# Writing expert results without a read-modify-write, and summing them in a last pass

## The reference

```python
h = tok(x, ...)                                   # 8 x 512 tokens, 192 features
h = h + attn(layernorm(h), ...)
h = h + ffn(layernorm(h), Wg, W1, b1, W2, b2)

def ffn(x, Wg, W1, b1, W2, b2):
    gate_scores = einsum('bsd,de->bse', x, Wg)
    topk_scores, topk_idx = top_k(gate_scores, 2)
    topk_probs = softmax(topk_scores)
    h = gelu(einsum('bsd,edh->bseh', x, W1) + b1)  # 8 experts, 384 hidden
    y = einsum('bseh,eho->bseo', h, W2) + b2
    y_sel = take_along_axis(y, topk_idx[..., None], axis=2)
    return sum(topk_probs[..., None] * y_sel, axis=2)
```

## Time and profile before

| what | value |
|---|---|
| median of 3 runs | 338.76 us (336.81 to 340.1) |
| span of the profiled execution | 338.6 us |
| POOL busy | 250.2 us (74%) |
| PE busy | 240.9 us (71%) |
| DVE busy | 177.6 us (52%) |
| ACT busy | 95.2 us (28%) |
| DMA moved | 22.61 MB |

### The profile page before, as it was taken

One profiled execution on the slowest core, in us unless ns is written; L12 is line 12 of the kernel. 1 busy time (PEld: TensorE's weight loads), 2 busy tenths in 40 slices (PEclk: granted clock), 3 DMA queues, 4 the chain that ended last, 5 costly groups with the idle time before them and its releaser, 6 DMA issues. The chain is left out here.

```text
span 338.6 us, 6221 instructions
## 1 busy us (share of the span) xinstructions
PE 240.9 (71%) x1585; PEld 162.0 (48%) x1585; DVE 177.6 (52%) x698; ACT 95.2 (28%) x223; POOL 250.2 (74%) x283
## 2 busy tenths in 40 slices
PE   0831973668478989768654899999999587999500
PEld 0621641223243445444421678777777365877400
DVE  5758997488998866684699322232222122122200
ACT  1002001354324144634233323332432132133000
POOL 5778979309968777766777388888883888888673
PEclk9999995558955556965555599999999799699955
DMA  6710019900000001111123146656461556564510
GB/s 191 201 13 11 0 45 400 382 5 2 2 0 9 12 13 60 63 57 60 59 70 103 22 54 69 64 62 67 53 69 18 60 62 65 61 69 50 59 10 0
DMA packets 28141, 22.61 MB, mean 67 GB/s; under 512 B 15434, under 2 KB 25546, under 8 KB 27787
## 3 DMA queue, kind: packets, MB, share of 16 engines
q0 software_dynamic: 13296, 7.95, 21.1%
q1 hardware_dynamic: 14524, 14.23, 13.0%
q10 hardware_dynamic: 288, 0.03, 0.1%
HBM read 7.25 MB, written 15.63 MB: 68 GB/s over the span
## 5 line engine op out<-in xcount | busy, mean ns | idle before, releaser
L709 POOL DMA_INDIRECT out<-up x71 | 110.3, 1554 | 33.1 <-issue 13.9
L1972 PE MATMUL bank_b<-down,up 128*128 x426 | 91.2, 354 | 5.0 <-DVE up L1473 1.0
L1972 PEld LDWEIGHTS bank_b<-down,up 128*128 128x128 f32 x426 | 72.9, 200 | 22.6 <-issue 18.8
L1473 DVE TENSOR_SCALAR up<-bank_b,up 128x192 f32<-128x192 f32 x71 | 29.6, 418 | 97.5 <-PE bank_b L1972 84.9
L657 POOL DMA_INDIRECT routed<-rows,slot x64 | 61.9, 968 | 23.9 <-issue 18.0
L472 POOL DMA_INDIRECT theta_all<-angles,ids x32 | 32.4, 1012 | 10.9 <-issue 9.0
L1651 ACT ACTIVATE up<-bank_a 128x384 f32<-128x384 f32 x71 | 31.3, 497 | 3.4 <-PE bank_a L1962 2.9
L1775 PE MATMUL bank_b<-queries_t,keys_t 32*128 32x512 f32 x64 | 26.1, 900 | 6.9 <-ACT keys_t L1499 3.4
L1782 PE MATMUL bank_a<-keys_t,wt 32*128 32x512 f32 x64 | 27.6, 949 | 3.8 <-DVE nmax L1133 2.1
L1663 ACT COPY up<-bank_c 128x384 f32<-128x384 f32 x18 | 8.6, 478 | 61.8 <-PE bank_c L1951 58.7
L1133 DVE TENSOR_REDUCE nmax<-bank_a 128x2 f32<-128x1024 f32 x16 | 19.5, 1219 | 11.5 <-PE bank_a L1782 11.3
(11 more groups left out here) (420 smaller groups left out, 369.4 us busy)
## 6 DMA issues: line engine op xcount, KB each, us to landing
routed<-pad_rows SPq DMA_DIRECT2D x8, 528.0 KB, 5.7
out<-hres SPq DMA_DIRECT2D x8, 384.0 KB, 2.4
down<-down_w SPq DMA_DIRECT2D x1, 2304.0 KB, 11.9
up<-up_w SPq DMA_DIRECT2D x1, 1536.0 KB
out<-up POOLq DMA_INDIRECT x71, 3.5
up<-routed SPq DMA_DIRECT2D x69, 16.0 KB
routed<-rows,slot POOLq DMA_INDIRECT x64
up<-up_w SPq DMA_DIRECT2D x1, 780.0 KB
```

The costliest lines, as they stand in the source:

```text
L709: pool.indirect_dma_start(out=out_rows, out_offset=bass.IndirectOffsetOnAxis(xb[:, m // STEP % RING, m % STEP, DEST:DEST + 1].bitcast(I32) ...
L1473: dve.tensor_scalar(y[:, m % RESULTS, :], bank_b[:, m % 2, 0:D], xb[:, m // STEP % RING, m % STEP, SHARE:SHARE + 1], None, ALU.mult).then_ ...
L1972: mm = pe.matmul(bank_b[:, m % 2, 0:D], hid[:, m % STEP, c * P:(c + 1) * P], down[:, bass.ds(first + c * D, D)], start=(c == 0), stop=(c = ...
```

## The change

The two rows of a token no longer meet in one place. A new buffer `results` in device memory has one row per token and choice (8192 rows), and 1024 spare rows for the rows of blocks that no token filled. POOL's DMA is a plain indirect write into it, with no add, no bounds check and no order between blocks. The destination that travels with a row is now `k * TOKENS + token`, and DVE takes the smaller of it and a spare row for each block (`target`, one column of 128 numbers). At the end SP loads all of `results` back, batch by batch (`back`, 16 transfers of 128 partitions by 768 numbers, 384 KB each), DVE adds the two rows and the residual (two additions of 128x768 per batch), and SP stores the batch. The stores of `hres` during attention are gone, since `out` is now written once, at the end.

The order computation on DVE is gone (18 instructions after the block table, and one in it). SP loads a block of the ring when DVE has scaled the old one (`y_done`), where it waited for the landing of that block's add. The circuits' tables move into the room of `back`, which is not used until the end; their instructions are the same. POOL has one more index table to fill early (`spare`).

```diff
             for m in range(BLOCKS):
-                last_shared = pool.value_load(t_i[0:1, 1, m:m + 1], min_val=1, max_val=BLOCKS + 1)
                 pool.wait_ge(y_done, m + 1)
-                pool.wait_ge(landed, last_shared)
-                hold(pool)
                 pool.indirect_dma_start(
-                    out=out_rows, out_offset=bass.IndirectOffsetOnAxis(
-                        xb[:, m // STEP % RING, m % STEP, DEST:DEST + 1].bitcast(I32), 0),
-                    in_=y[:, m % RESULTS, :], in_offset=None, bounds_check=TOKENS - 1,
-                    oob_is_err=False, compute_op=ALU.add).then_inc(added[m % RESULTS], 16)
+                    out=results, out_offset=bass.IndirectOffsetOnAxis(target[:, m % RESULTS:m % RESULTS + 1], 0),
+                    in_=y[:, m % RESULTS, :], in_offset=None).then_inc(added[m % RESULTS], 16)
...
             def weighted(m):
                 dve.wait_ge(y_mm, m + 1)
                 if m >= RESULTS:
                     dve.wait_ge(added[m % RESULTS], 16 * (m // RESULTS))
+                dve.tensor_tensor(target[:, m % RESULTS:m % RESULTS + 1],
+                                  xb[:, m // STEP % RING, m % STEP, DEST:DEST + 1].bitcast(I32),
+                                  spare[:, m % RESULTS:m % RESULTS + 1], ALU.min)
...
+            dve.wait_ge(h2_copied, 2 * BATCHES)
+            for b in range(BATCHES):
+                dve.wait_ge(back_in[b], 32)
+                step(dve.tensor_tensor(back[:, b, 0, :], back[:, b, 0, :], back[:, b, 1, :], ALU.add))
+                join()
+                dve.tensor_tensor(hres[:, b, :], hres[:, b, :], back[:, b, 0, :], ALU.add).then_inc(summed, 1)
...
-            for m in range(BLOCKS):
-                sp.wait_ge(added[m % RESULTS], 16 * (m // RESULTS) + 16)
-                sp.sem_inc(landed, 1)
-                if m + RING * STEP < BLOCKS:
-                    load_block(m + RING * STEP, block_row(m + RING * STEP))
-            sp.wait_ge(h2_out, 16 * BATCHES)
+            for m in range(BLOCKS - RING * STEP):
+                sp.wait_ge(y_done, m + 1)
+                load_block(m + RING * STEP, block_row(m + RING * STEP))
+            for n in range(RESULTS):
+                sp.wait_ge(added[n], 16 * len(range(n, BLOCKS, RESULTS)))
+            for b in range(BATCHES):
+                for k in range(2):
+                    sp.dma_start(back[:, b, k, :], results_view[b, k]).then_inc(back_in[b], 16)
+            for b in range(BATCHES):
+                store(b)
+            sp.wait_ge(sum_out, 16 * BATCHES)
```

More of the change, by code:

```diff
@@ L77, in build @@
     ids_view = token_ids.rearrange("b (p j) -> p b j", j=TILES)
-    out_rows = out.rearrange("b s d -> (b s) d")
     out_view = out.rearrange("b (p j) d -> b p (j d)", j=TILES)
+    results = nc.dram_tensor("results", (2 * TOKENS + RESULTS * P, D), F32, kind="Internal").ap()
+    results_view = results[0:2 * TOKENS, :].rearrange("(k b p j) d -> b k p (j d)", k=2, b=BATCHES, j=TILES)
     ctx = ExitStack()
@@ L89, in build, with behind @@
         ids = sb("ids", [P, BATCHES, TILES], I32)
-        theta_all = sb("theta_all", [P, T, ANGLES])
-        angle_stages = sb("angle_stages", [P, 3, CT, ANGLES])
+        back = sb("back", [P, BATCHES, 2, TILES * D])
+        circuit_room = [back[:, :, :, :].rearrange("p b k x -> p (b k x)"), 0]
+        def behind(room, pattern, **sizes):
+            size = int(np.prod(list(sizes.values())))
+            room[1] += size
+            assert room[1] <= room[0].shape[1]
+            return room[0][:, room[1] - size:room[1]].rearrange(pattern, **sizes)
@@ L99, in build @@
[L99 to L122, removed]
+        def table(*dims):
+            return behind(circuit_room, "p (x t) -> p (x t)", x=int(np.prod(dims)), t=CT), dims
@@ new lines, in build @@
+        bloch = table(QUBITS, 8)
+        turn = table(QUBITS, 3)
+        turn_s = table(QUBITS)
+        step_m = table(QUBITS - 2, 8)
+        chain = table(QUBITS, 16)
+        chain_q = table(4, 2, 2, 2)
+        ends = table(6)
+        tails = table(6)
+        parity = table(QUBITS - 1, 2)
+        pair_b = table(QUBITS - 2, 2, 3)
+        pair_e = table(QUBITS - 1, 9)
+        pair_s = table(QUBITS - 1, 2)
+        pair_d = table(QUBITS - 1, 3)
+        first_h = table(4)
+        first_w = table(2)
@@ L124, in build @@
+        last_r = table(9)
+        last_t = table(8)
+        last_v = table(2)
+        last_2 = table(6)
+        last_a = table(3, 4)
+        last_c = table(2, 8)
+        z_exp = table(QUBITS)
+        z_tmp = table(2, QUBITS - 1)
+        x_exp = table(QUBITS)
         ev = sb("ev", [P, T, F])
@@ L173, in build @@
         up_room_1 = [up1[:, :, :].rearrange("p e h -> p (e h)"), 0]
[L174 to L179, removed]
+        angle_room = [angle_stages.rearrange("p a t f -> p (a t f)"), 0]
         down = sb("down", [P, E * HC * D])
@@ L184, in build @@
         ge = behind(angle_room, "p (e m) -> p e m", e=E, m=BLOCKS)
-        ge_w = behind(angle_room, "p (h e m) -> p h e m", h=2, e=E - 1, m=BLOCKS)
+        ge_w = behind(angle_room, "p (h e m) -> p h e m", h=1, e=E - 1, m=BLOCKS)
         var1_p = sb("var1_p", [P, CT, PU])
@@ L231, in build @@
         need = sb("need", [P, RING], I32)
-        seen = sb("seen", [P, 2, E])
-        shared_last = sb("shared_last", [P, 3, E - 1])
-        first_late = sb("first_late", [P, E - 1])
+        spare = sb("spare", [P, RESULTS], I32)
+        target = sb("target", [P, RESULTS], I32)
         cum = sb("cum", [P, 2, E])
@@ L349, in build @@
         added = [sem(f"added{n}") for n in range(RESULTS)]
-        landed = sem("landed")
+        back_in = [sem(f"back_in{b}") for b in range(BATCHES)]
+        summed = sem("summed")
+        sum_out = sem("sum_out")
         passed = sem("passed")
@@ L410, in store @@
             def store(b):
-                sp.wait_ge(h2_copied, 2 * b + 2)
-                sp.dma_start(out_view[b], hres[:, b, :]).then_inc(h2_out, 16)
+                sp.wait_ge(summed, b + 1)
+                sp.dma_start(out_view[b], hres[:, b, :]).then_inc(sum_out, 16)
             def block_row(m):
@@ L424, in rows_written @@
                 hold(sp)
[L426 to L430, removed]
-            sp.sem_inc(landed, 1)
+            sp.wait_ge(scattered_last, 16)
+            sp.sem_inc(first_marked, 1)
             sp.wait_ge(table_done, 1)
```

54 lines of the change are left out of this document (10 added, 44 removed).

## The result

The changed kernel takes **335.27 us** (median of 6 runs, 334.54 to 336.5) and the kernel before 338.5 us (median of 6, 336.81 to 340.1) on the same chip. The ratio is **0.9901, with a 95% interval of 0.9874 to 0.9929**: about 1% faster, where 0.7% slower was forecast. Run again later beside other kernels it gave 0.9874 (0.9834 to 0.9913). The profiled execution took 334.54 us, with a span of 332.7 us.

A forecast was written before the change was run, and what follows sets the result against it. POOL was taken to pace the experts at 1.86 us per block, PE close behind at 1.627. Last write seen at 310.2 us, plus 27 us of tail and 3.8 us of end, gave 341.0 us (+0.7%), range 334 to 349 us.

The forecast's parts named there:

- The end: From the last landing to the span's end: 3.9 us before, kept at 3.8 us.
- signs that the prediction gave for being wrong: POOL's line 709 over 1.33 us, PE's pace moving from 1.63 us, or holes in the tail's DMA share.
- POOL's DMA: POOL's plain indirect write in the expert part: 0.96 us instead of 1.55 us, like the short-row write.
- Rival 1: POOL's write in the expert part keeps 1.55 us and POOL stays the bound: 358 to 361 us, chance 0.16.
- The expert stretch: First to last scaling: PE sets 1.627 us per block, so the last scaling starts 11.9 us earlier, at 306.3 us.
- The start does not move: Start of the first scaling: the 6.1 us of order computation removed from DVE lie under cover, since scaling waits for PE.
- The new tail: After the last write: 16 loads and 8 stores, 9.44 MB, bound by transfers, 27 us; DVE's additions beside them.
- Rival 2: In the tail, gaps open between loads and stores in one queue: 30 to 35 us, 344 to 349 us total, chance 0.10.
- Rival 3: In the tail, loads and stores overlap: tail 22 us, total 336 us, 333 us at the shortest; chance 0.12.

The follow-up runs named there:

- cover: The kernel before with one 384 KB load of finished output added behind SP's last wait; ratio 0.9996 to the kernel before.
- late_dma: The changed kernel with one more indirect write on POOL after the tail's last store has landed; ratio 1.0158 to the kernel before, span 342.0 us.
- late_memset: The changed kernel with one memset on POOL after the tail's last store has landed, no transfer behind it; run once, span 342.3 us.
- before_noadd: The kernel before with the accumulation taken from POOL's indirect writes, bounds check kept, sums missing from the output; ratio 0.9415 to the kernel before, span 317.4 us.
- before_again: The kernel before, run once more with nothing changed; 339.36 us, span 337.6 us, first scaling at 191.9 us.
- bf16: The changed kernel with row buffer, scaled rows and tail loads in bfloat16, each loaded row added to the residual directly; 329.07 us, ratio 0.9678 to the kernel before.
- early2: The changed kernel with tail loads waiting only for blocks that hold rows, the counts read ahead by SP; 330.4 us, ratio 0.9764 to the kernel before.
- sorted: The changed kernel with lower-numbered experts' rows in the first half of `results`, each half's loads waiting for its own block counts; 335.1 us, ratio 0.9894 to the kernel before.

## Why the prediction was wrong

The step that failed is **"The end": "From the last landing to the span's end it took 338.6 - 334.7 = 3.9 us before; I keep it at 3.8."** It was 0.4 us. The 3.9 us were not a fixed cost behind the last landing. SP, done at 335.0 us, waited in them for POOL's DRAIN. The change takes POOL off the end and puts 26 us of transfers behind it, so the DRAIN is hidden. The row was there to read: a wait of 3.5 us on SP in line 82, and a DRAIN on POOL that starts at 328.5 us and lasts 9.8 us. I read the distance and not its cause, and none of the signs that the prediction gave for being wrong looks at the end. cover shows that this time was open to other work, late_dma and late_memset that it comes back as soon as POOL is last.

From the first scaling on, the forecast was 341.0 - 193.1 = 147.9 us and the profile has 143.1 us, a miss of 4.8 us:

| step | forecast | measured |
|---|---|---|
| price of POOL's write | 0.96 us | 0.959 us |
| first scaling to end of last | 113.7 us | 113.4 us |
| from there to SP's first load | 3.4 us | 3.1 us |
| tail, first load to last landing | 27 us | 26.2 us |
| the end | 3.8 us | 0.4 us |

So the exit is 3.4 of the 4.8 us, and with it the sign: before has 145.6 us from the first scaling on, the forecast is 2.3 above that and the measurement 2.5 below; with 0.4 us for the end the forecast would have been 1.1 below.

- **"POOL's DMA"** was right, and for the reason that the nearest row gave: the plain write costs what the short-row write costs, and before_noadd puts 568 ns on the adding. Rival 1 falls.
- **"The expert stretch"** was right: 113.0 us for 70 blocks is 1.614 us per block (1.627 forecast), PE's clock at 1.00 throughout. Its sentence "The start does not move" can't be held against one profile: 189.6 us here against 193.1, most of which goes with the granted clock of the attention (before_again). That is the other 3.5 us between 341.0 and 332.7 us.
- **"The new tail"** was right in kind and 0.8 us too dear, but its parts missed more than their sum, in opposite directions. Transfers move 413 GB/s once the engines are full, above the 358 to 399 GB/s of the earlier trace rows: 9.44 MB at that rate is 22.9 us, not 24.2. Beyond that the tail has 3.3 us, not 1.4: the first 6 us at 239 GB/s alone lose 2.5 us. That 27 us came out so near is partly luck. The HBM Reference of the Trainium skill (Specifications (TRN2)), which I used for a core's share of 358 GB/s, also says in that section that a core streaming alone reaches some 425 GB/s, bounded by its DMA engines; the 413 GB/s at a share of 1.03 agree with this second sentence, and the first did not bind.
- **Rival 2** (gaps between loads and stores) falls: from 312 us on, where the loads pass into stores, the share is 1.03, and the 2.5 us lie ahead of the first store (314.86 us). **Rival 3** comes nearest in time, 336 - 193.1 = 142.9 us from the first scaling on against 143.1, but by luck: its tail of 22 us was 26.2, and its end of 3.8 us was 0.4. Its mechanism is not borne out: loads and stores do not overlap for free, since leaving the loads and additions out gives 16.4 us, and the loads' 6.29 MB take 15.2 us at 413 GB/s.
- **The basis** was off too. I compared a span of 341.0 us with a span of 338.6 us and took the latter for the median. The runs take 1.7 to 2.1 us more than their spans (339.36 us for a span of 337.6 us in before_again), so the span shown belonged to one of the longer runs, with the latest first scaling of all traces.

Of the 3.2 us between the two medians, 2.2 us lie behind the first scaling (145.6 to 143.4 us, means of the two kernels' profiles) and are explained. The other 1.0 us, found by difference, lies ahead of it, where four traces of the old code have the first scaling at 192.2 us in the mean and six of the new one at 190.8 us; how much of it is the clock and how much the change is open, with 0.3 to 0.7 us between old and new code where the clock was alike.

## What to carry to other kernels

Before keeping the time between the last landing and the span's end as a constant, look at which engine's DRAIN the others wait for there: here it was POOL's, 7.2 us behind a plain write or a memset (4.8 us behind an accumulating write), and it costs nothing if other work ends later. An accumulating indirect write cost its issuing engine 0.57 us more per 128 rows here than a plain one, and the kernel had to keep an order between writes to a shared row; but taking the adding out of it moves its bytes into a pass of their own, and that pass takes its bytes' time at the full rate of the DMA engines (413 GB/s here) unless it is begun under the compute or made smaller.

## What the runs showed of the hardware

- POOL's price for an indirect write of 128 rows doesn't depend on the row's length: 957 ns for rows of 384 bytes (bf16), 959 ns for 768 bytes, 958 ns for 128 bytes.
- POOL's closing DRAIN follows a memset of 0.16 us, 29 us after its last DMA, with the same 7.2 us as behind a plain indirect write. In early2, where large loads had been issued ahead of POOL's last write, it was longer: 304.69 to 313.55 us, 8.9 us.
- SP needed some 0.63 us for one count that it reads from on-chip memory between two waits; eight of them held sorted's second loads for 5 us.
- Large loads beside POOL's row writes ran at 280 GB/s in all with the DMA engines busy at 0.92 (early2, 300 to 306 us); the first 6 us of the changed kernel's loads alone at 239 GB/s (0.73); large loads and stores together at 413 GB/s (1.03).
